# The sum over four bilinear corners: one strided reduction or two additions

## What is computed

```python
def corner(yi, xi, wgt):
    valid = (yi >= 0) & (yi < Hh) & (xi >= 0) & (xi < Ww)
    idx = (jnp.clip(yi, 0, Hh - 1) * Ww + jnp.clip(xi, 0, Ww - 1)).reshape(Bb, DG, -1)
    v = jnp.take_along_axis(xg, idx[:, :, None, :], axis=3)
    return v * (wgt * valid).reshape(Bb, DG, 1, -1)
val = corner(y0i, x0i, (1 - fy) * (1 - fx)) + corner(y0i, x0i + 1, (1 - fy) * fx) + corner(y0i + 1, x0i, fy * (1 - fx)) + corner(y0i + 1, x0i + 1, fy * fx)
...
g = deform_sample(x, py, px) * mask[:, :, None]
wr = dc_w.reshape(dc_w.shape[0], DG, Cc // DG, K)
out = jnp.einsum('odck,bdckhw->bohw', wr, g)
```

## Time and profile before

| | us |
|---|---|
| median of 3 timed runs | 4010.8 |
| lowest, highest | 4009.16, 4013.34 |
| the profiled execution (its span) | 4500.8 |
| first gather issued, last gather issued (start) | 2854.4, 4438.5 |
| DVE busy | 3169.4 (70%) |
| POOL busy | 907.3 (20%) |

### The profile page before, as it was taken

How to read it: one execution, slowest core, us unless ns; L and a number is a source line. 1 busy time by engine, 2 the same in 40 slices (tenths; PEclk the granted TensorE clock), 3 DMA queues, 4 the chain that set the end, 5 groups by cost and what they waited for, 6 DMA issues and landing times. The chain is left out here.

```text
span 4500.8 us, 58636 instructions
## 1 busy us (share of the span) xinstructions
PE 3405.0 (76%) x22186; PEld 1347.4 (30%) x22186; DVE 3169.4 (70%) x3652; ACT 2843.2 (63%) x2698; POOL 907.3 (20%) x974
## 2 busy tenths in 40 slices
PE   3777559999999999999999998447556655674445
PEld 2454333233333333333334343112112212221111
DVE  5999768999999984999999994234435444444445
ACT  1444326999999994999999992234434444443444
POOL 2000010000000000000000000445554554545452
PEclk7656569999999999999999998757767777776667
DMA  2200000000000000000000000211211111121110
GB/s 43 89 1 1 1 3 1 1 1 1 1 1 2 2 1 1 1 1 1 1 1 2 2 1 13 52 34 38 54 41 38 47 46 33 43 54 39 39 41 21
DMA packets 117631, 89.65 MB, mean 20 GB/s; under 512 B 96496, under 2 KB 98576, under 8 KB 117340
## 3 DMA queue, kind: packets, MB, share of 16 engines
q0 software_dynamic: 28672, 58.78, 4.7%
q1 hardware_dynamic: 87036, 26.32, 2.6%
q10 hardware_dynamic: 1632, 0.56, 0.1%
HBM read 65.61 MB, written 19.96 MB: 19 GB/s over the span
## 5 line engine op out<-in xcount | busy, mean ns | idle before, releaser
L1556 ACT ACTIVATE adder_layer_Z<-adder_layer_CP,AN 128x2048 f32 x984 | 1873.3, 2013 | 33.4 <-PE PS L1517 32.6
L1517 PE MATMUL PS<-adder_layer_Z,c_adder_out 128*32 128x512 f32 x16896 | 1845.0, 593 | 57.9 <-ACT adder_layer_Z L1556 33.1
L1602 DVE TENSOR_SCALAR adder_layer_Z<-adder_layer_CP,AW 128x2048 f32 x1128 | 1369.9, 1281 | 45.5 <-PE PS L1517 31.5
L1517 PEld LDWEIGHTS PS<-adder_layer_Z,c_adder_out 128*32 128x32 f32 x16896 | 649.6, 110 | 1253.0 <-issue 1176.1
L1973 POOL DMA_INDIRECT sampler_G<-neighbours,sampler_IDX x896 | 849.6, 948 | 834.9 <-DVEq L2039 436.9
L2260 ACT ACTIVATE sampler_HY<-PS,G_hat 128x512 f32<-128x512 f32 x512 | 309.0, 686 | 319.6 <-PE PS L2139 119.6
L1609 DVE SCALAR_TENSOR_TENSOR adder_layer_Z<-adder_layer_CP,AW,adder_layer_Z 128x1024 f32<-128x1024 f32 x384 | 476.4, 1282 | 35.6 <-issue 35.6
L2148 PE MATMUL PS<-sampler_HXM,G_spread 32*128 32x512 f32 x128 | 99.1, 864 | 387.4 <-DVEq L2065 341.9
L2063 DVE TENSOR_TENSOR P<-sampler_HY,PS 128x2048 f32<-128x2048 f32 x64 | 146.4, 2287 | 338.9 <-remote 255.3
L2262 ACT ACTIVATE sampler_HY<-sampler_HY 128x2048 f32<-128x2048 f32 x128 | 244.6, 1911 | 8.7
L1474 POOL MEMSET XP<- 128x4624 f32 x1 | 4.0, 3952 | 1046.4 <-PE PS L1533 1046.4
(11 more groups left out here) (376 smaller groups left out, 3018.8 us busy)
## 6 DMA issues: line engine op xcount, KB each, us to landing
sampler_G<-neighbours,sampler_IDX POOLq DMA_INDIRECT x896
neighbours<-top_k_zero SPq DMA_DIRECT2D x16, 578.0 KB, 7.2
neighbours<-sampler_HT SPq DMA_DIRECT2D x256, 32.0 KB, 1.7
X<-in_x SPq DMA_DIRECT2D x8, 256.0 KB, 6.3
out<-X SPq DMA_DIRECT2D x8, 256.0 KB
P<-in_L_conv_conv_w SPq DMA_DIRECT2D x4, 144.0 KB
P<-in_L_conv_add_w SPq DMA_DIRECT2D x4, 144.0 KB
RAW<-in_L_conv_w SPq DMA_DIRECT2D x4, 144.0 KB
```

The source lines that it names most:

```text
L1517: mm = t.matmul(PS[32 * j:32 * j + 32, k, :], K["adder_out"][:, 32 * i:32 * i + 32], Z[:, r % SLOTS, j, c:c + BANK], start=False, stop=Fal ...
L1556: op = a.activation(z(r, j), seen(ch, ty, tx), ACT.Relu, bias=ANf[:, weight(ty, tx, j, i)])
L1602: op = v.tensor_scalar(z(r, j), seen(ch, ty, taps[0]), AWf[:, weight(ty, taps[0], j, i)], 0.0, ALU.subtract, ALU.max)
```

## The change

In `sample` the reduction over the corners, whose innermost direction steps over 32 elements, becomes two additions: corners 0 and 1 plus corners 2 and 3, in place in `G`, then the first 32 elements plus the next 32, into `VAL`. The wait for a free `VAL` buffer moves behind the first addition and a drain.

```diff
--- before.py
+++ after.py
@@ -2031,10 +2031,11 @@
                         g3 = gt[:, :, :].rearrange("p k (q c) -> p (k q) c", q=4)
                         v.tensor_tensor(g3, g3, WP.unsqueeze(2).broadcast_to([128, GK * 4, CG]), ALU.mult)
                         v.drain()
+                        v.tensor_tensor(gt[:, :, 0:2 * CG], gt[:, :, 0:2 * CG], gt[:, :, 2 * CG:4 * CG], ALU.add)
+                        v.drain()
                         if th >= 2:
                             v.wait_ge(t_ps, th - 1)
-                        v.tensor_reduce(VAL[:, th % 2, :, :], gt[:, :, :].rearrange("p k (q c) -> p k c q", q=4),
-                                        AX.X, ALU.add)
+                        v.tensor_tensor(VAL[:, th % 2, :, :], gt[:, :, 0:CG], gt[:, :, CG:2 * CG], ALU.add)
                         v.drain().then_inc(val, 1)
                         v.sem_inc(used, 1)
```

## The result

The changed kernel takes 4045.7 us (median of 4 runs, 4044.8 to 4048.1) against 4012.1 us (4 runs, 4009.2 to 4013.4) of the kernel before: a ratio of 1.0085, 95% interval 1.0073 to 1.0097. It is 33.6 us slower, although VectorE (DVE) has less to do. The forecast was 4039 us.

The account below looks back on a forecast made before the run. POOL issuing gathers back to back was taken as the bound: 4010.8 + 29.6 us of gathers' waits - 1.5 us at the end = 4038.9, so 4039 us, range 3990 to 4063.

Parts of the forecast that it names:

- POOL as the bound: Sampler: POOL issues 14 gathers a step back to back, 17.5 us a step, and so bounds the timed runs.
- floor: Time that POOL's gathers alone set, from first gather to end of span: 4003.9 us, 6.9 us under the timed median.
- DVE's saving: Two additions and a drain replace a 3.265 us reduction: 1.47 us a step less, 94 us in all, hidden beside POOL.
- The gathers' wait: A gather waits until DVE's two-SBUF-input first addition ends: 0.47 us a step (0.15 to 0.85), 29.6 us over 63 steps.
- input point: Moment about 0.13 us after a gather's start when it wants its input and waits if DVE then holds it.
- The tail's 1.5 us: Last step, whose gathers are all issued: DVE's shorter work takes 1.5 us off the end.
- Rival 1: Gathers don't wait for the new additions; only the last step's 1.5 us remains: 4009.3 us, chance 0.14.
- Rival 3: Compute chain bounds the timed runs, so steps give back up to 1.47 us: 3917 us at most, chance 0.22.
- compute chain: DVE and its partners in a sampler step: 14 us at most without stalls, 3.5 us less than POOL's 17.5.
- what I expected of the changed kernel's profile: Gathers' mean near 0.97 us, POOL's wait for L2039 lower, profiled span perhaps tens of microseconds shorter.

Follow-up runs that it names:

- before_again: The kernel before, with no edit, profiled once more: 4014.1 us, with a span of 4012.3 us.
- psum_operand: The changed kernel with each addition replaced by a product of the same shape whose second input is in PSUM: 4011.9 us, ratio 0.9994 to the kernel before.
- extra_896_sbuf: The kernel before plus a maximum of 896 elements per step between multiplication and reduction, both inputs in SBUF: 4046.1 us, ratio 1.0079.
- extra_896_psum: The kernel before plus a multiplication of 896 elements per step between multiplication and reduction, second input in PSUM: 4016.1 us, ratio 1.0002.
- ten gathers: Both kernels with 10 instead of 14 gathers a step: 3927.9 us for the kernel before, 3891.5 us for the changed one.

## Why the prediction was right

**POOL as the bound.** Right. It was an inference from a sum (floor 4003.9 us, median 4010.8), made against the page, which showed POOL waiting. `before_again` shows the sum's picture directly: no wait for `used`, 144.7 us of waits by DVE.

**DVE's saving.** Right: 1.09 + 0.63 us predicted, 1.094 + 0.625 measured, and worth nothing (`psum_operand`, 0.9994). The pieces with gaps cost as much an element as contiguous ones.

**The gathers' wait.** Right in that a gather waits for the addition to end, in the 0.13 us to be taken off, and nearly in size. The mis-sized term is 0.47 us a step: measured, it is 33.7 / 63 = 0.53. The step shown above has the predicted value, 0.48; the rest comes from steps in which the data arrived or DVE started later, so that more of the addition was left at the gather's start. Of the 62 waits nearly all lie between 0.4 and 0.75 us, three near 0.9. The reading of the 0.13 us as an input point was wrong, as the two steps above show; it changed no term, since in the usual phase the addition starts well before the gather. The sum with 0.53 is 4010.8 + 33.7 - 1.5 = 4043. The tail's 1.5 us was measured as 1.3: from the last gather's start to the end of DVE's last instruction it is 26.1 us in `before_again` and 24.8 in the changed kernel.

**Rival 1** (no wait, by the inference of the Trainium skill's page SBUF — State Buffer, section Who interferes with whom, that tensor_tensor leaves descriptor generation alone) fell: with the same length and place, the second SBUF input costs 30 us (`extra_896_sbuf` against `extra_896_psum`). The other sentence of that page of the Trainium skill, that two SBUF inputs contend with a GpSimd instruction that reads SBUF, agrees with the 0.48 us in the step shown.

**Rival 3** (the compute chain bounds) fell for this kernel and holds with ten gathers, at 36 of the 94 us that it was priced at.

**What was wrong.** Besides the input point three statements, none of them in the sum. The compute chain was put at 14 us a step at most; `before_again` gives 17.5 - (144.7 - 22.2) / 63 = 15.6 us (22.2 us is the wait for the very first data). The slack over DVE was thus 1.9 us a step and not 3.5, and `extra_896_psum`, with 1.17 us more DVE work a step, came close to using it up: DVE waits for data 55.9 us in all there. Second, what I expected of the changed kernel's profile supposed that it would have the stalls of the page before: a mean gather of 0.97 us, a smaller wait for L2039, a span shorter by tens of microseconds. It had none of these stalls, so the mean rose to 0.988 us (885.5 / 896) and the wait for `used` vanished. Third, the price of rival 3 counted DVE's saving in full, where with ten gathers 57 of 98 us turned into waits for PE and ACT.

## What to carry to other kernels

When GpSimd issues indirect gathers back to back, look at what VectorE is running as each one starts. In this kernel a `tensor_tensor` with two SBUF inputs held a gather up until about its end, and so did `tensor_scalar` instructions with one; a reduction and a `tensor_tensor` with its second input in PSUM didn't. So neither the length of the VectorE work nor the count of its inputs alone tells it; the trace does. Ask first whether the issuing engine or VectorE is the bound; the same two additions cost 34 us in the one case and gave back 36 us in the other. And set the profiled span beside the timed runs before any wait on the page is believed: here the page's largest waits were not in the timed runs, and a floor summed from undisturbed rows said so.

## What the hardware showed that I had not expected

The first profile of the kernel before spans 490 us more than its timed runs, with all of the excess in the sampler; a second one of the same kernel spans 4012.3 us against a run of 4014.1. No other profile of this study has the long form. Further, the size of the gathers' wait follows one rule over DVE instructions of four lengths (0.62, 0.69, 1.09 and 2.03 us): their end after the gather's start, less 0.11 to 0.14 us. And it is a matter of who comes first: an addition that starts 0.05 us before the gather costs it 0.91 us, one that starts 0.04 us before it costs it nothing and is itself 0.07 us longer.
